# First layer of a two-layer recurrent kernel: VectorE takes the low halves and the gate factor ahead of the scan of the values, and TensorE turns the gated sums back one block of matmuls later

## What is computed

```python
xs = jnp.pad(x, ((0, 0), (1, 0), (0, 0)))[:, :-1]
xm = x * time_mix + xs * (1.0 - time_mix)          # x is xn here
k = jnp.exp(jnp.minimum(einsum('btc,dc->bdt', xm, Wk), 60.0))
v = einsum('btc,dc->bdt', xm, Wv)
r = einsum('btc,dc->btd', xm, Wr)
kv = k * v
wkv = _depthwise_causal_conv(kv, w, T, C)          # w: a geometric decay, the newest tap apart
wk = _depthwise_causal_conv(k, w, T, C) + 1e-09
s = (jax.nn.sigmoid(r) * swapaxes(wkv / wk, 1, 2)) @ Wo.T
h = jnp.concatenate([x, -x], axis=-1)
h = relu(s0 * h @ W0) * 2; h = relu(s1 * h @ W1) * 2; g = s2 * h @ W2    # W0, W1, W2 are +1 or -1
x = x + s * silu(g)
```

## Time and profile before

| | us |
|---|---|
| runs of the kernel before: 672.5, 672.55, 673.92; median | 672.55 |
| the profiled execution, whole | 672.1 |
| its span in the trace | 670.3 |
| TensorE busy | 629.5 (94%) |
| VectorE busy | 601.0 (90%) |
| ScalarE busy | 511.4 (76%) |
| GpSimd busy | 280.1 (42%) |

### The profile page before, as it was taken

How to read it: one execution, slowest core, us unless ns; L and a number is a source line. 1 busy time by engine, 2 the same in 40 slices (tenths; PEclk the granted TensorE clock), 3 DMA queues, 4 the chain that set the end, 5 groups by cost and what they waited for, 6 DMA issues and landing times. The chain is left out here.

```text
span 670.3 us, 9285 instructions
## 1 busy us (share of the span) xinstructions
PE 629.5 (94%) x2714; PEld 304.2 (45%) x2714; DVE 601.0 (90%) x1406; ACT 511.4 (76%) x794; POOL 280.1 (42%) x275
## 2 busy tenths in 40 slices
PE   4779999999999998799999999999999999999986
PEld 2334444444444443344545444454444544444442
DVE  4999999999999999988988988898898899889856
ACT  2846666666666665889988898898888889899886
POOL 6556777777777765222123032122313303221220
PEclk9999999999999999999999999999999999999999
DMA  7331000000000000000000000000000000000000
GB/s 178 109 94 31 1 0 1 1 0 1 0 2 1 0 1 1 1 0 1 16 1 17 17 4 14 16 17 0 17 17 1 17 17 17 0 18 17 0 17 32
DMA packets 10770, 11.65 MB, mean 17 GB/s; under 512 B 4800, under 2 KB 6288, under 8 KB 10720
## 3 DMA queue, kind: packets, MB, share of 16 engines
q1 hardware_dynamic: 9744, 10.73, 5.3%
q0 software_dynamic: 112, 0.33, 0.1%
q10 hardware_dynamic: 864, 0.00, 0.1%
HBM read 6.87 MB, written 4.19 MB: 16 GB/s over the span
## 5 line engine op out<-in xcount | busy, mean ns | idle before, releaser
L1150 PE MATMUL bank<-arena,w 128*128 128x512 f16 x640 | 148.6, 379 | 4.1 <-DVE arena L774 4.1
L1150 PE MATMUL bank<-arena,dnT 128*128 128x512 f32 x288 | 138.6, 592 | 0.0
L435 POOL TENSOR_TENSOR arena<-arena 128x512 f32<-128x512 f32 x48 | 59.7, 1271 | 137.6 <-ACT arena L590 137.6
L650 ACT ACTIVATE arena<-bank,xinv 128x512 f32<-128x512 f32 x144 | 94.4, 693 | 24.9 <-PE bank L1150 24.6
L1150 PEld LDWEIGHTS bank<-arena,w 128*128 128x128 f16 x640 | 62.5, 98 | 78.3 <-issue 10.1
L482 ACT ACTIVATE arena<-bank 128x512 f16<-128x512 f32 x96 | 53.8, 606 | 35.8 <-PE bank L1150 35.8
L425 POOL TENSOR_TENSOR arena<-arena 128x512 f32<-128x512 f32 x16 | 16.8, 1050 | 140.6 <-DVE arena L1011 140.6
L1150 PEld LDWEIGHTS bank<-arena,dnT 128*128 128x128 f32 x288 | 53.7, 191 | 35.9 <-issue 24.4
L1150 PE MATMUL bank<-arena,wsqT 128*128 128x512 f32 x128 | 64.6, 609 | 5.3 <-DVE arena L783 5.3
L1020 DVE SCALAR_TENSOR_TENSOR arena<-bank,cws,arena 128x506 f32<-128x506 f32 (+1 forms) x96 | 67.1, 740 | 1.1
L774 DVE SCALAR_TENSOR_TENSOR arena<-bank,arena 128x512 f16<-128x512 f32 x96 | 60.3, 671 | 2.4 <-ACT arena L482 1.2
(11 more groups left out here) (221 smaller groups left out, 1492.6 us busy)
## 6 DMA issues: line engine op xcount, KB each, us to landing
x_all<-in_L_attn_x SPq DMA_DIRECT2D x16, 256.0 KB, 2.6
out<-x_all SPq DMA_DIRECT2D x16, 256.0 KB, 2.0
up_n<-in_L_ffn_routed_up SPq DMA_DIRECT2D x1, 512.0 KB, 3.7
dn_n<-in_L_ffn_routed_down SPq DMA_DIRECT2D x1, 512.0 KB, 5.3
wx<-in_L_attn_W_x SPq DMA_DIRECT2D x1, 288.0 KB, 2.9
k_u<-in_L_ffn_k POOLq DMA_DIRECT2D x1, 256.0 KB, 5.8
w_in<-in_L_attn_W_in SPq DMA_DIRECT2D x1, 256.0 KB, 2.7
k_u<-in_L_ffn_k SPq DMA_DIRECT2D x1, 128.0 KB, 6.1
```

Source lines behind the costliest of these rows:

```text
L435: g.tensor_tensor(prod[:, c, :], act[:, c + 1, :], gate[:, :], ALU.mult).then_inc(sem["b_actp"], 1)
L650: a.activation(act[:, c, :], up_bank(f, c)[:, :], ACT.Gelu, scale=xinv[:, I_UP:I_UP + 1]).then_inc(sem["b_act"], 1)
L1150: return nc.tensor.matmul(ps, lhsT, rhs, start=start, stop=stop)
```

## The change

VectorE, turns 1 to 15: the four `low(0, f, j)` and `gp` move ahead of the scan of the values, `sg` stays behind it. So the run scan of keys, scan of values, four low halves, gp, sg becomes scan of keys, four low halves, gp, scan of values, sg. TensorE, turns 2 to 15: `turn_back` moves from between `hidden1(m, 0)` and `hidden1(m, 1)` to behind both. No instruction is added, removed or resized, no wait is changed, and ScalarE, GpSimd and SyncE keep their streams.

```diff
                 if f == 1:
                     largest()
+                if has(f) and f != 0:
+                    low(0, f, 0)
+                    low(0, f, 1)
+                    low(0, f, 2)
+                    low(0, f, 3)
+                if has(m):
+                    dve.wait_ge(sem["a_thf"], m + 1)
+                    after(dve, sem["a_sg"], m)
+                    v.scalar_tensor_tensor(gp[:, :], thf[:, :], 1.0, b_F[:, :], ALU.add, ALU.mult).then_inc(sem["a_gp"], 1)
                 if has(f):
                     dve.wait_ge(sem["a_kv"], f + 1)
...
                     last.then_inc(sem["a_scanV"], 1)
-                if has(f) and f != 0:
-                    low(0, f, 0)
-                    low(0, f, 1)
-                    low(0, f, 2)
-                    low(0, f, 3)
-                if has(m):
-                    dve.wait_ge(sem["a_thf"], m + 1)
-                    after(dve, sem["a_sg"], m)
-                    v.scalar_tensor_tensor(gp[:, :], thf[:, :], 1.0, b_F[:, :], ALU.add, ALU.mult).then_inc(sem["a_gp"], 1)
+                if has(m):
                     dve.wait_ge(sem["a_gp"], m + 1)
...
                     hidden1(m, 0)
+                if has(m):
+                    hidden1(m, 1)
                 if has(t):
                     pe.wait_ge(sem["a_sg"], t + 1)
...
                     turn_back(b_RX).then_inc(sem["a_sgT"], 1)
-                if has(m):
-                    hidden1(m, 1)
```

More of the change, by code:

```diff
@@ L831, in layer0 @@
                     largest()
[L832 to L838, removed]
                 if has(f) and f != 0:
@@ L847, in layer0 @@
                     v.scalar_tensor_tensor(gp[:, :], thf[:, :], 1.0, b_F[:, :], ALU.add, ALU.mult).then_inc(sem["a_gp"], 1)
+                if has(f):
+                    dve.wait_ge(sem["a_kv"], f + 1)
+                    after(dve, sem["a_wkv"], f)
+                    for s in range(SEQ):
+                        last = v.tensor_tensor_scan(Pv[:, s, 1:], dec[:, :], kv[:, s * T:(s + 1) * T], 0.0,
+                                                    ALU.mult, ALU.add)
+                    last.then_inc(sem["a_scanV"], 1)
+                if has(m):
                     dve.wait_ge(sem["a_gp"], m + 1)
```

## The result

The changed kernel takes 676.1 us (median of 7 runs, 675.08 to 678.37), the kernel before 672.55 (7 runs, 671.28 to 673.94). The ratio is 1.0052, 95% interval 1.0034 to 1.0069: slower by 0.5%, some 3.5 us. The forecast was 673.7 with a range of 669.5 to 677.0: the time lies in the range and on the forecast's side of the kernel before, but the loss is three times the 1.2 us that I had worked out. The profiled execution after took 678.17 us (span 676.4), 2 us above its median; before it was 672.1 (span 670.3). So a difference of the two traces is larger than that of the medians.

A forecast was written before the change was run, and what follows sets the result against it. A ring through four engines set the pace, and after the change VectorE alone would close it. Turns 3 to 14, 1, 2 and 15 (+1.7 - 0.2 + 0.54 - 0.7, taken as +1.2) on 672.55 gave 673.7 us, range 669.5 to 677.0.

The forecast's parts named there:

- The ring: Turns 3 to 14: a dependency loop through VectorE, GpSimd, TensorE and ScalarE sets the pace; 15.52 us becomes 15.65 to 15.69.
- the hold-ups: Two-input VectorE instructions and GpSimd reads of SBUF exclude each other; `ekm` 0.79 to 0.42 us, L367 1.21 to 1.04.
- the pair: The two scans of the values on VectorE, now beside L410: 1.25 to 2.19 us, the second waiting for L410.
- R: End of the second reciprocal on VectorE in a turn; the next `xm` was forecast 8.18 us after it, against 7.64.
- Turn 1: Low halves and `gp` end earlier, the scan falls on GpSimd's chain: -0.2 us, bounds -0.6 and +0.6.
- Turn 2: No held-up `ekm` to relieve here, only the longer tail before the next `xm`: +0.54 us.
- Turn 15: `ek` earlier and scans meeting an idle GpSimd, partly offset by L413 and L416: -0.7 us, bounds -1.5 and 0.
- The sum: Whole kernel: +1.7 - 0.2 + 0.54 - 0.7 = +1.3 us, taken as +1.2.
- Rival 1: L410 starts before the scans in each turn: `xm` later, 15.86 us a turn, +3.9 us, 676.4; chance 0.17.
- Rival 3: No hold-up where the scan now stands; `gp` waits for `thf`: 15.15 us a turn, -5.5 us, 667; chance 0.08.
- Rival 2: Second scan gets in ahead of L410, which is late instead: 15.42 us a turn, -2.2 us, 670.3; chance 0.12.
- the gain of 0.37 us in `ekm`: Middle turns: moving `turn_back` ends L400 earlier, so `ekm` falls from 0.79 to 0.42 us and `xm`-to-reciprocal from 7.88 to 7.51.

The follow-up runs named there:

- experiment 3: Changed kernel with GpSimd's L410 (sum of k) replaced by a memset that reads nothing: 668.19 us, ratio 0.9923.
- experiment 5: Changed kernel with GpSimd's two sums swapped, wkv (L413's work) ahead of wk (L410): 673.67 us, ratio 1.0021.
- experiment 7: Changed kernel with `gp` moved back behind the scan of the values, next to `sg`: 683.56 us, ratio 1.016.
- experiment 4: Changed kernel with VectorE's old order in turn 1 alone: 673.76 us, ratio 1.0002.
- experiment 1: Kernel before with VectorE's new order alone, `turn_back` staying between the two chunks of `hidden1`: 683.78 us, ratio 1.0145.
- experiment 9: Changed kernel with VectorE's old order in turn 1, wkv ahead of wk, and `ysr` (L416) moved into GpSimd's next turn behind `ekm`: 665.96 us, ratio 0.9892.
- experiment 2: Kernel before with TensorE's move of `turn_back` alone, VectorE keeping its old order: 691.0 us, ratio 1.0267.
- experiment 10: Kernel before with one wait added, keeping GpSimd's second low half (L400) behind `ekm`: 693.15 us, ratio 1.0287.

## Why the prediction was right, and where it was not

**The ring and the hold-ups: right.** `ekm` 0.79 to 0.41, L367 1.21 to 1.04, the pair 1.25 to 2.20, `xm` at R+8.12 (R+8.18 foretold), TensorE idle 0.70 (0.75), the turn 15.62 (15.65 to 15.69). Twelve turns cost 1.2 us by the starts of `xm` (187.46 against 186.27) where I put 1.7. Experiments 3 and 5 show the cause of the pair, experiment 7 that the same reading carries over to another position.

**Turn 1: the term that was mis-sized.** I took -0.2 us, with bounds of -0.6 and +0.6 for one hold-up more or less. It was +1.9 in the trace, of which 1.2 go with the order (experiment 4) and about 0.7 with the clock. The step that failed is the count of hold-ups behind the scan. Up to `sg` the new order won 0.9 us, as the sign of the term says. But four of the small setup operations fell on operations of GpSimd (0.60, 1.22, 0.93 and 1.00 us), 3.1 us more than without a hold-up; in the kernel before it was two (0.61 and 1.05 us), 1.3 us more. To see that, every operation behind `sg` has to be walked along GpSimd's rows, and not one of them.

**Turn 2: near by luck in the trace, right by experiment 4.** It was +0.4 instead of +0.54, but not by the forecast way: behind the late `xm` and the low clock VectorE waited 0.31 us for a high half, L410 started before the scans and kept 1.19 us, and the pair took 1.57 us. In experiment 4, with a clock of 1.00 there, the pair took 2.20 us and the turn +0.51 against before, which is the forecast.

**Turn 15: right up to the second layer, then given back.** From `xm` to the first statistics behind `sg` it took 14.65 us (264.26 - 249.61) instead of 16.16 (261.53 - 245.37): -1.5, the full gain. An operation behind them (0.46 us before) was held up by L416 as foretold. VectorE in the changed kernel, in that passage:

```profile
265.45 1.20 DVE L908 TENSOR_SCALAR w_inH<-w_in,wsc 128x512 f16<-128x512 f32 x1
...
275.41 0.69 DVE L774 SCALAR_TENSOR_TENSOR arena<-bank,arena 128x512 f16<-128x512 f32 x1 [0.87 <-ACT arena L482]
```

The second row is the part that I did not have: TensorE waited 2.0 us for the normalised rows of the second layer, its granted clock then fell (0.73 on average from 270 to 275 us), and the high half that VectorE wants came late by 0.87 us. I took -0.7 for the whole passage; it was +0.2 in this trace. In the trace of experiment 4 TensorE waited 2.0 us at the same place, the clock stayed at 1.00, and the same stretch took 26.7 us (248.68 to 275.34), -0.8 against before.

**The sum.** The terms that go with the order are +1.2 (turns 3 to 14), +1.2 (turn 1), +0.5 (turn 2) and -0.8 (turn 15): +2.1 us, where I had +1.3. The medians are 3.5 us apart. Not shown, but in line with the runs, is that most of the rest is the granted clock: its mean was 0.986 to 0.994 in the seven runs of the changed kernel, and at least 0.995 in 44 of the 49 runs of the kernel before beside the experiments. The prediction had no term for it.

**The rivals.** None took the place of the forecast. Rival 1 is real, and experiment 1 shows it: there TensorE's lead is shorter and the scan is issued behind L410's start. Rival 3, without hold-up, gave the turn of experiments 3 and 9 to 0.01 us, in part by luck: it had `gp` waiting for `thf` in each turn, and the rows show turns of two lengths, with 0.15 us of waiting for `xh` ahead of one `xm` and 0.47 us for a high half in the next turn. Rival 2, the second scan ahead of L410, was seen nowhere. What no rival had is the late state of experiments 2 and 10: I took the gain of 0.37 us in `ekm` for a gain of the ring in any order of VectorE. In the changed kernel it is one, because the low halves that TensorE waits for stand ahead of the scan. That is what VectorE's new order does for the kernel; the price is the scan beside L410.

## What to carry to other kernels

Where two engines exclude each other, a turn has to be read as a pair of time tables: price a moved instruction by the ends of the other engine's operations at its new place, and walk every instruction behind it along that table, small ones too. A gain on one engine can end in a later meeting and a slower steady state (0.37 us won, 1.5 us lost a turn), so shorten a ring only together with what it will then run into. And if an engine has to wait for a result anyway, put that wait ahead of its other large work: with wkv ahead of wk GpSimd stood idle for 1.3 to 2.1 us and the pair of scans took 1.26 us.

## What the runs showed of the hardware

- The opening says that an engine waits on another only at a semaphore. Between VectorE and GpSimd that does not hold here: no semaphore stands between L410 and the scans of the values, and both take longer side by side (1.57 and 2.20 us) than apart (1.18 and 1.25).
- A memset of 128x512 by GpSimd (0.53 us) beside a scan of VectorE leaves the pair at 1.27 us; an addition of the same shape (1.18 us alone) takes 1.57 there and stretches the pair of scans from 1.25 to 2.20 us.
- Operations of one column are held up like large ones: a `tensor_tensor` of 128x1 took 1.22 us instead of 0.16, and a `tensor_scalar` of 128x7 took 1.00 instead of 0.16.
- Steady states depend on phase: the same instructions, with one wait more, settle at 17.0 instead of 15.5 us a turn, and stay there for all the turns left.
- TensorE's granted clock fell to 0.66 to 0.73 over 5 us at places where it had been idle for about 2 us, in some executions and not in others; one stretch of turn 1 varied by 0.7 us with it. Behind the idle stretches of 3.25 to 4.32 us at the head of turn 2 it fell in all five traces that have them.
